# Four of sixteen states fed by channel, the first step on two PSUM banks, and a longer list of weight places at the end

## The reference

```python
u  = conv(x @ in_proj) + conv_b             # 256 channels, 4 taps
dt = clip(sigmoid(u @ dt_w.T + dt_b), 1e-4, 1)
B, C = u @ B_w.T, u @ C_w.T                 # 16 values of each per token
for t in tokens_of_a_sequence:              # state: 256 channels x 16
    dA = exp(clip(dt * A, -5, 5))
    state = dA * state + dt * u * B + 1e-6  # "the input" is the last two terms
    y = sum(state * C, states) + D * u
x = x + (y * silu(z)) @ out_w.T
n = layernorm(x)
x = x + shared_expert(n) + sum of the top 2 of 8 routed experts, weighted
```

## Time and profile before

| | us |
|---|---|
| median of 3 runs | 1420.82 (1420.7, 1420.82, 1425.83) |
| the profiled execution, its own time | 1425.94 |
| its span, first to last instruction | 1424.1 |
| start, to the first scan | 45.9 |
| the 256 units, first to last scan | 1257.7 |
| end, after the last scan | 120.5 |
| DVE busy over the span | 1177.5 (83%) |
| PE busy over the span | 1233.5 (87%) |
| ACT busy / POOL busy over the span | 899.6 (63%) / 845.9 (59%) |

### The profile page before, as it was taken

The page is one execution under the profiler, slowest core; times in us unless marked ns, Lnnn a source line. Parts: engine busy times, 40 slices in busy tenths (PEclk is TensorE's granted clock), DMA queues, the critical chain, the costliest instruction groups (busy, mean ns, idle before and its releaser), DMA issues.

```text
span 1424.1 us, 27089 instructions
## 1 busy us (share of the span) xinstructions
PE 1233.5 (87%) x8709; PEld 1033.9 (73%) x8709; DVE 1177.5 (83%) x2236; ACT 899.6 (63%) x1450; POOL 845.9 (59%) x1354
## 2 busy tenths in 40 slices
PE   5788888888989898998989898998989899897884
PEld 3566766677777777787777777787777778786773
DVE  0499999988898979998898979988898979897322
ACT  2775756567577767677676767677676767761221
POOL 3435553754557773867657773867657773665344
PEclk9699999999999999999999999999999999999897
DMA  5000000032323242243313242243312233266672
GB/s 175 1 1 8 1 9 1 27 115 65 115 59 95 84 138 80 67 128 98 119 58 95 84 134 83 67 128 94 122 58 86 93 124 103 79 193 204 201 242 80
DMA packets 110653, 132.28 MB, mean 93 GB/s; under 512 B 10032, under 2 KB 81584, under 8 KB 110384
## 3 DMA queue, kind: packets, MB, share of 16 engines
q1 hardware_dynamic: 102320, 113.73, 25.7%
q0 software_dynamic: 8192, 16.79, 4.0%
HBM read 102.37 MB, written 28.11 MB: 92 GB/s over the span
## 4 chain that ended last, share of the span: by engine, by line
PE 40%; DVE 28%; issue 13%; ACT 10%; POOL 6%; DMA 2%; SPq 1%; DVEq 0%; POOLq 0%; ACTq 0%
DVE h L1201 12%; DVE yT L1219 11%; PE p_hT L1000 7%; PE p_db L983 6%; PE p_misc L1032 5%; PE p_dn L1146 5%; PE p_gu L1134 3%; PE p_gu L1125 3%; PE p_misc L1043 3%; POOL xs_dram L740 2%; ACT L931 2%; ACT dA L835 2%; ACT hm L931 2%; PE p_misc L1026 2%; PE p_misc L1069 1%
## 5 line engine op out<-in xcount | busy, mean ns | idle before, releaser
L1201 DVE TENSOR_TENSOR_SCAN h<-dA,p_db 128x512 f32<-128x512 f32 x512 | 602.5, 1204 | 74.7 <-PE p_db L983 46.5
L698 POOL TENSOR_SCALAR dBT<-wT,bcT 128x256 f32<-128x256 f32 x704 | 339.3, 482 | 346.8 <-ACT wT L865 139.4
L1219 DVE SCALAR_TENSOR_TENSOR yT<-p_hT,bcT,yT 128x256 f32<-128x256 f32 x960 | 402.7, 471 | 31.0 <-PE p_hT L1000 30.9
L983 PE MATMUL p_db<-ident,dBT 128*128 128x128 f32 x2048 | 300.6, 280 | 58.3 <-DVE h L1201 52.0
L835 ACT ACTIVATE dA<-dt_sb,A_sb 128x510 f32<-128x510 f32 x512 | 332.8, 711 | 28.4 <-DVE h L1201 27.2
L983 PEld LDWEIGHTS p_db<-ident,dBT 128*128 128x128 f32 x2048 | 239.7, 144 | 107.4 <-issue 95.8
L1000 PE MATMUL p_hT<-ident,h 128*128 128x128 f32 x2048 | 292.2, 282 | 25.9 <-DVE yT L1219 17.0
L1000 PEld LDWEIGHTS p_hT<-ident,h 128*128 128x128 f32 x2048 | 239.1, 145 | 66.5 <-DVE yT L1219 30.8
L740 POOL DMA_INDIRECT xs_dram<-xn,slot x128 | 127.1, 993 | 69.6 <-issue 33.9
L891 ACT ACTIVATE dBT<-wT,eps,bcT 128x256 f32<-128x256 f32 x320 | 163.9, 592 | 0.1
L754 POOL DMA_INDIRECT ysel<-ys_dram,slot x128 | 123.5, 965 | 65.2 <-issue 32.6
(11 more groups left out here) (153 smaller groups left out, 1478.3 us busy)
## 6 DMA issues: line engine op xcount, KB each, us to landing
wring<-w_moe_dram SPq DMA_DIRECT2D x177, 384.0 KB, 4.3
xt<-xs_dram SPq DMA_DIRECT2D x41, 256.0 KB, 5.0
ys_dram<-yo SPq DMA_DIRECT2D x41, 256.0 KB, 2.3
dA<-w_moe_dram SPq DMA_DIRECT2D x14, 384.0 KB, 4.8
x_sb<-x_dram SPq DMA_DIRECT2D x16, 256.0 KB, 4.3
out_dram<-x SPq DMA_DIRECT2D x16, 256.0 KB, 2.4
xs_dram<-ysel SPq DMA_DIRECT2D x4, 512.0 KB, 5.8
xs_dram<-xn,slot POOLq DMA_INDIRECT x128, 2.3
```

Of the source, the lines that this page charges most:

```text
L698: op = pool.tensor_scalar(dBT[:, j % DBT_RING, c], wT[:, g % 2, c], bcT[:, g % 2, c, n:n + 1], STATE_EPS, ALU.mult, ALU.add)
L983: mm = pe.transpose(p_db[half][:, c * P:(c + 1) * P], dBT[:, j % DBT_RING, c, half * P:(half + 1) * P], ident[:])
L1201: dve.tensor_tensor_scan(h[:, j % 2, half], dA[:, j % DA_RING, half], p_db[half][:], 0.0, ALU.mult, ALU.add).then_inc(scan_done, 1)
L1219: op = dve.scalar_tensor_tensor(yT[:, g % 2, cc], p_hT[pair][:, c], bcT[:, g % 2, cc, NS + n:NS + n + 1], yT[:, g % 2, cc], ALU.mult, ALU.add)
```

## The change

Three edits in one.

1. **Four states by channel.** `KINDS` goes from `pppsspspppppppss` (11 p, 5 s) to `psdsdsdsdpppppps` (7 p, 5 s, 4 d). For a d state nothing is turned by PE: the 16 values of B of each token are turned once for a group (name br: 4 transposes of 128x16 into `p_misc`, an ACT copy to `bc_sb`), stored to DRAM (R), and for each d state SP loads its row of 512 values back, spread over all 128 partitions (b, 256 KB in SBUF, 2 places). POOL multiplies it with `w_sb`, one instruction of 128x1024 in SBUF; ACT adds 1e-6 in place, one instruction of 128x1024 (name e); DVE scans with both inputs in SBUF. `dBT` goes from 3 places to 2, `xn2T` from 4 to 3, the lead of x from 4 units to 3.
2. **The first step.** Products for group 0 take `p_misc` and `p_dn` in turn. The tap weights are loaded in four parts with a semaphore each, `chan` before them, and the first exponentials stand ahead of wT and z.
3. **The end.** Weight places for the last tiles: 12 outside the ring (8 in `dA`, 2 in `dBT`, 2 in `dt_sb`), taken first, and 8 in the ring. Loads of weights and tiles are put 4 slots ahead of their quad, not 3 and 2. After the last step ACT issues the stores of expert results, not SP. The last group is combined and stored chunk by chunk.

All slot tables are written anew; of them the diff below shows the start of ACT's first step. Its core:

```diff
-KINDS = "pppsspspppppppss"
+KINDS = "psdsdsdsdpppppps"
-DBT_RING = 3
+DBT_RING = 2
+DBS_RING = 2
+ROW_RING = 2
+ROW_LEAD = 7
+EPS_LEAD = 2
-EXP_LEAD = 4
+EXP_LEAD = 3
-  "xnT u0", "u1 dt0", "dt1 bc", "wT0 wT1", "x x x z0 z1 d", "x d V X E", "x d V X E",
+    "xnT u0", "u1 dt0", "dt1 bc br", "x x x x x x x x x x x x x x", "wT0 wT1", "d e", "d e", "d e", "d e",
...
-TAIL_WEIGHT = 3
+ACT_STORES = NS * GROUPS
+TAIL_FETCH = 4
-WEIGHT_LEAD = 2
+WEIGHT_LEAD = 4
-LOAD_LEAD = 5
+LOAD_LEAD = 6
-SPARE = 8
+SPARE = 10 + DBT_RING * CHUNKS * CH // WROW
+        def misc_bank(name, g):
+            if misc_at[name, g] in at_start and misc_at[name, g] % 2:
+                return p_dn[:].rearrange("p c d -> p (c d)")
+            return p_misc[:]
@@ sync
+            def store_rows(g):
+                sp.wait_ge(misc_emptied, misc_at["br", g])
...
+                sp.dma_start(bc_rows[g % 2], bc_sb[:]).then_inc(rows_stored, 16)
+            def load_row(j):
...
+                at_least(sp, dbs_by_pool, at - ROW_RING + 1)
+                sp.dma_start(brow[:, at % ROW_RING], bc_rows[g % 2, n:n + 1].broadcast_to([P, TOK])
+                             ).then_inc(row_loaded[at % ROW_RING], 16)
@@ gpsimd, state_input
+                if KINDS[n] == "d":
+                    at = of_kind("d", j)
+                    pool.wait_ge(row_loaded[at % ROW_RING], 16 * (at // ROW_RING + 1))
+                    at_least(pool, scan_done, 2 * unit_of("d", at - DBS_RING) + 2 if at >= DBS_RING else 0)
+                    pool.tensor_tensor(dBs[:, at % DBS_RING], w_sb[:], brow[:, at % ROW_RING].rearrange(
+                        "p (o t) -> p o t", o=1).broadcast_to([P, HALVES, TOK]), ALU.mult).then_inc(dbs_by_pool, 1)
@@ scalar
+            def add_eps(j):
...
+                act.wait_ge(dbs_by_pool, at + 1)
+                act.activation(dBs[:, at % DBS_RING], dBs[:, at % DBS_RING], ACT.Identity, bias=eps[:]
+                               ).then_inc(dbs_ready, 1)
@@ tensor
+                if kind == "d":
+                    return
+                if name == "br":
+                    pe.wait_ge(misc_emptied, misc_at["bc", g])
+                    for c in range(CHUNKS):
+                        mm = pe.transpose(bank[0:NS, c * P:(c + 1) * P], bcT[:, g % 2, c, 0:NS], ident[:])
@@ vector, scan_state
+                if KINDS[j % NS] == "d":
+                    dve.wait_ge(dbs_ready, at + 1)
+                    source = dBs[:, at % DBS_RING, half]
@@ vector, the last group
+                for c in range(CHUNKS):
+                    dve.wait_ge(last_loaded[c], 32)
+                    for j in range(2):
+...
                        dve.scalar_tensor_tensor(x1[:, g % X1_RING, c], ysel[:, j, c], weight[:, b % ROUTE_RING, j, cc:cc + 1],
                                                 x1[:, g % X1_RING, c], ALU.mult, ALU.add).then_inc(last_comb, 1)
```

238 lines of the change are left out of this document (175 added, 63 removed), and 44 rows, old and new, of tables (ACT_FIRST, ACT_SLOTS, DVE_SLOTS, PE_FIRST).

## The result

The changed kernel takes 1440.6 us (median; 1437.7 to 1446.7) against 1420.7 us (1416.1 to 1425.8) for the kernel before on the same chip. The ratio is 1.0149, with a 95% interval of 1.0116 to 1.0181. So it is 1.5% slower, which is less than 2% but clear of the noise; 1380 us was predicted. The profiled execution took 1446.7 us, with a span of 1445.0: it is the slowest of the five, 6.1 us above their median, as that of the kernel before is 5.1 above its own.

What follows compares the result with a forecast made beforehand. PE was taken to bound the half of each group where convolution, dt and output projection crowd in, DVE the other half. Units -26, start -8 and end -7 gave -41 us, hence 1380 us, range 1347 to 1422.

Steps and rivals of the forecast that it cites:

- Start and end: First step and the stretch after the units: start -7.8 us (bounds -3 and -10), end -7 us (bounds -1.7 and -14).
- Taken from PE: Crowded half of each group: fewer transposes free PE of net 57.0 us, 3.6 a group, all taken as gain before costs.
- nothing (DVE as the next bound): Lower bound of the gain from PE's removed transposes: no gain; the upper bound was about 77.4 us.
- Put on ACT: Additions of 1e-6 and copies on ACT in the units: 82 us more work, taken as hidden.
- 75% busy, hidden: ACT over the units: 82 us on 860.5 in 1257.7 leaves it 75% busy, so the added work costs nothing.
- if the cover were gone: Price of ACT's added work in the units were it not hidden: 5 us a group.
- The lock: d scans with two SBUF inputs wait for POOL's instruction under way: 61 us, half hidden, 30.6 us remaining.
- B: In the units DVE becomes the bound, blocked scans wholly unhidden, leaving start and end: 1406 to 1410 us; chance 0.17.
- C: POOL becomes the bound in the crowded half, in every second group: 1440 to 1450 us; chance 0.12, half in force 0.09.
- A: Lock on d scans seldom met or absorbed by remaining waits; 72 us go, up to 80: 1345 to 1352; chance 0.18.
- D: PE's granted clock falls to 0.95, crowded halves grow 1 us each: 16 us, 1396; chance included in the forecast's 0.44.
- three signs by which the forecast was to be wrong: d scans all 1.2 us; DVE idle under 50 us with units still 1250; DVE's waits naming POOL or ACT's dBs.

Runs made afterwards that it cites:

- e1: Kernel before with only the new start and end, its units unchanged: 1404.1 us, 0.9891 of before.
- e5: e1 with 2 PE transposes instead of 8 for states 2, 4, 6 and 8, from the second group on: 1398.8 us, 0.9853 of before.
- e6: Changed kernel with 16-column products, no addition of 1e-6, and d scans reading PSUM: 1374.3 us, 0.9688 of before.
- e10: Changed kernel with 16-column products and d scans reading PSUM, ACT's addition of 1e-6 kept: 1399.7 us, 0.9868 of before.
- e4: Changed kernel without ACT's addition of 1e-6, scans waiting for POOL's product directly: 1407.7 us, 0.9929 of before.
- e2: Changed kernel with the d states' scans reading PSUM instead of SBUF, product and addition still made: 1404.6 us, 0.9901 of before.
- e3: Changed kernel with POOL's product on 16 of 1024 columns, the others holding zero: 1402.8 us, 0.9891 of before.
- e9: Changed kernel without the addition of 1e-6 and with d scans reading PSUM, POOL's full product kept: 1378.3 us, 0.9709 of before.
- E: ACT's addition of 1e-6 as the only one of the three costs left in, the kernel of e10: 1399.7 us.
- e8: Changed kernel with the addition of 1e-6 one unit later in ACT's order: 1430.7 us, 1.0087 of before.
- e18: Changed kernel with state 5's input multiplied on POOL instead of ACT: 1490.3 us, 1.0072 of before; changed kernel on the same chip 1489.3 us.

## Why the prediction was wrong

**Start and end: right.** -8.9 and -8.1 us in the trace of the changed kernel, and 14.4 us between the medians of e1's comparison (1418.5 to 1404.1), where 14.8 were forecast. The first scan at 37.0 and an end of 112.4 answer to the forecast 38 and 113.

**Taken from PE: the first error, some 27 us.** The step that failed is "I take all of it as gain before the costs". It rested on the earlier trace rows, where PE is busy 33.04 of 35.40 us in the crowded half. e5 shows that the relief in the old order is worth 5 us, and e6 that relief, lighter POOL and new order together are worth 30, against 57. An engine busy 93% of a stretch in which another waits for it is not yet the bound: part of the waiting must belong to something else, by the timelines a sequence through ACT and POOL. The wait for p_db in the earlier trace rows did go; DVE then waited for the output projection instead. The lower bound of the term, "nothing (DVE as the next bound)", was nearly what e5 gives, for another reason.

**Put on ACT: the second error, some 33 us.** The step is "75% busy, hidden". The size was right (1.14 us an addition, ACT 72% busy over the units), and the cover was not there, since 75% was a mean over all units. In group 8 two of the four additions, at 668.98 and 675.55, stand in units 2 to 4, where the new order has ACT nearly without a gap even when there are no additions, as e6's windows show. The additions cost 25 us with nothing else there (e10) and 33 with everything (e4 against the changed kernel), some of it through PE's clock. The forecast's own price "if the cover were gone", 5 us a group, is 80 us, too much; measured are 2.

**The lock: right in mechanism, and in size by two errors that cancel.** Forecast were 61 us of blocked scans with half of them hidden, 30.6. Measured are 38 us of blocked scans and 36 us for the lock as it stands in the changed kernel (e2): fewer scans are blocked, and almost none of it is hidden. Without the long products the lock costs 5 us. The Trainium skill (SBUF — State Buffer, "Who interferes with whom"), on which the term leaned, says that a DVE instruction with two SBUF inputs contends with a GpSimd instruction that reads SBUF. The traces agree, with 3.37 us for a scan beside a product and 1.22 at most once an operand is in PSUM (e2). By the reading in which it would have been 0, e2 would have changed nothing.

**Sum.** Units by the forecast: -57 + 30.6 + 0. By the runs, with the costs in the order addition, then product and lock: -30 + 25 + 33 + 8 for what they do to each other = +36, and 1404 + 36 = 1440. In the 8 the clock may stand: unit 8 of five groups at 0.81, 5 x 1.64 = 8 us, occurs in the changed kernel and in none of e2, e3 and e4.

**The rivals.** B had the right thought, that the gain is taken back, but priced only DVE. C had the right time, 1440 to 1450, and half the right carrier: its words were that POOL becomes the bound in the crowded half, in every second group. The loss is in every second group, and the late product holds ACT in its queue, which the forecast named and kept for this rival. But POOL's load is not the bound by itself: e9, with the full products, costs 4 us, and e10, with 16 columns of each, 25. A did not come, since the d scans are blocked. D came true, 0.95 against 0.98 in the earlier trace rows; e6 has 0.97 and e1 0.98. It is not a rival to the other costs but comes with them: over units 2 to 4 of the even groups the clock is 1.00 with none of the costs, 0.95 with E and 0.93 with all. What it costs is 1.64 us in a unit 8 that has it, as shown at e8; over the whole kernel it was not measured. A's own arithmetic was off: 72 to 80 us from 1420.8 give 1341 to 1349 us.

None of the three signs by which the forecast was to be wrong came: the d scans don't all take 1.2 us, DVE is idle for 125.9 us and not under 50, and its waits name PE, with 1.8 us for ACT's dBs. A load on an engine behind PE shows in DVE's waits as PE.

**What stays open.** Whether the addition costs by its load or by its place. e8 says that a later place gives 10 us net, e10 that load without any product to wait for costs 25, and e18 that taking other work from ACT does not help when POOL gets it. An addition that costs neither engine anything in units 2 to 4 was not tried. The share of the new order of slots in e6's 30 us was not separated from the relief either, nor how much of the loss goes through PE's clock beyond unit 8.
